# Routed experts: one accumulation array in DRAM, or two by tile parity with a sum at the end

## The reference

```python
x = x + xattn(layernorm(x), ctx_2048, Wq, bq, Wkv, bkv, Wp, bp)
flat = layernorm(x).reshape(-1, D)
scores = sqrt(softplus(flat @ router_w.T))
_, idx = top_k(scores + expert_bias, 4)
topv = take_along_axis(scores, idx, 1); topv /= topv.sum(-1) + 1e-20
probs = zeros((T, E)).at[arange(T)[:, None], idx].set(topv)
for wg, wu, wd, p in experts:
    out += p[:, None] * clamped_swiglu(flat, wg, wu, wd)
out += clamped_swiglu(flat, shared_gate_w, shared_up_w, shared_down_w)
x = x + out
```

## Time and profile before

| | |
|---|---|
| median of 3 runs | 1599.62 us |
| the profiled execution, its own time | 1606.57 us |
| its span, first to last instruction | 1604.8 us |
| mean granted TensorE clock | 0.919 |
| busy: TensorE matmul, VectorE, ScalarE, GpSimd | 83%, 65%, 53%, 53% of the span |
| DMA | 221.56 MB, mean 138 GB/s |

### The profile page before, as it was taken

One profiled execution on the slowest core, in us unless ns is written; L12 is line 12 of the kernel. 1 busy time (PEld: TensorE's weight loads), 2 busy tenths in 40 slices (PEclk: granted clock), 3 DMA queues, 4 the chain that ended last, 5 costly groups with the idle time before them and its releaser, 6 DMA issues.

```text
span 1604.8 us, 28516 instructions
## 1 busy us (share of the span) xinstructions
PE 1335.0 (83%) x7922; PEld 664.3 (41%) x7923; DVE 1036.9 (65%) x1863; ACT 851.7 (53%) x1183; POOL 855.4 (53%) x772
## 2 busy tenths in 40 slices
PE   7997787778778777887877659889988998989996
PEld 3443333344344444443443334444444444444443
DVE  6456789999999999999999827623323233332331
ACT  2223699888899888898998931112211111111221
POOL 1001477677777777777776710535444444444451
PEclk9999689898898899889898969999999999999999
DMA  7332466665666556566666647276767656666455
GB/s 225 86 72 59 73 119 125 112 119 113 129 136 130 120 118 121 118 127 131 131 115 111 115 166 250 84 229 161 198 181 213 189 129 190 162 192 129 88 93 165
DMA packets 383109, 221.56 MB, mean 138 GB/s; under 512 B 344801, under 2 KB 344929, under 8 KB 378786
## 3 DMA queue, kind: packets, MB, share of 16 engines
q1 hardware_dynamic: 365186, 177.36, 45.4%
q0 software_dynamic: 17872, 43.58, 14.3%
HBM read 103.42 MB, written 36.70 MB: 87 GB/s over the span
## 4 chain that ended last, share of the span: by engine, by line
DVE 26%; PE 25%; issue 22%; DMA 19%; ACT 4%; POOL 2%; DVEq 1%; POOLq 0%; SPq 0%; ACTq 0%
DMA acc_dram<-mem 16%; DVE mem L540 15%; PE psS L750 10%; PE psS L758 4%; DVE mem L570 3%; PE psS L434 3%; PE psAV L405 2%; PE psS L1559 2%; DMA mem<-xn_dram,mem 1%; ACT mem L493 1%; PE psT L1187 1%; PE psP L1540 1%; DMA mem<-xn_dram 1%; DVE mem L516 1%; PE psP L742 1%
## 5 line engine op out<-in xcount | busy, mean ns | idle before, releaser
L625 POOL TENSOR_SCALAR mem<-mem 128x2048 bf16<-128x2048 uint8 x256 | 485.4, 1901 | 183.6 <-DMA mem<-mem 161.5
L493 ACT ACTIVATE mem<-mem 128x2048 uint8<-128x2048 f32 x256 | 536.3, 2095 | 12.4
L434 PE MATMUL psS<-mem 128*128 128x512 bf16 x1024 | 351.6, 430 | 158.4 <-DVE mem L570 114.5
L750 PE MATMUL psS<-mem 128*128 (+1 forms) x752 | 358.4, 620 | 0.0
L570 DVE TENSOR_SCALAR_CACHE_REDUCE mem<-psS,mem 128x1024 f32<-128x1024 f32 x256 | 328.2, 1282 | 23.9
L540 DVE TENSOR_SCALAR_CACHE_REDUCE mem<-psS 128x1024 f32<-128x1024 f32 x256 | 311.9, 1218 | 18.6 <-PE psS L434 18.5
L778 ACT ACTIVATE mem<-mem 128x256 f32<-128x256 f32 x94 | 39.3, 418 | 368.2 <-DVE mem L784 368.2
L1157 POOL DMA_INDIRECT acc_dram<-mem x78 | 125.4, 1607 | 195.5 <-DVE mem L1257 152.3
L784 DVE TENSOR_SCALAR mem<-psS 128x512 f32<-128x512 f32 x94 | 65.0, 692 | 220.9 <-PE psS L750 219.4
L434 PEld LDWEIGHTS psS<-mem 128*128 128x128 bf16 x1024 | 74.2, 103 | 317.2 <-DVE mem L540 146.9
L750 PEld LDWEIGHTS psS<-mem 128*128 128x128 f32 x752 | 141.6, 199 | 149.5 <-issue 147.4
(11 more groups left out here) (207 smaller groups left out, 1253.8 us busy)
## 6 DMA issues: line engine op xcount, KB each, us to landing
mem<-in_moe_w SPq DMA_DIRECT2D x33, 1536.0 KB, 9.4
mem<-in_x SPq DMA_DIRECT2D x32, 256.0 KB, 2.9
acc_dram<-mem SPq DMA_DIRECT2D x29, 256.0 KB, 2.3
mem<-mem SPq DMA_TRANSPOSE x288, 3.1
xn_dram<-mem SPq DMA_DIRECT2D x17, 256.0 KB, 2.1
mem<-in_ctx_in SPq DMA_DIRECT2D x16, 256.0 KB, 3.2
mem<-xn_dram SPq DMA_DIRECT2D x16, 256.0 KB, 4.4
mem<-acc_dram SPq DMA_DIRECT2D x16, 256.0 KB, 4.3
```

Of the source, the lines that this page charges most:

```text
L434: last = nc.tensor.matmul(psS[c][:, k * D:(k + 1) * D], qT[p][:, h, :], kT[:, h, c * HALF + k * D:c * HALF + (k + 1) * D], start=True, sto ...
L493: nc.scalar.activation(p8[slot], S[slot], ACT.Exp, bias=NB[:, slot:slot + 1], scale=sq[p][:, h:h + 1], accum_out=Z[p][:, h:h + 1]).then_in ...
L625: nc.gpsimd.tensor_scalar(pb[slot], pT[slot].bitcast(U8).rearrange("p (j q b) -> p j b q", b=2, q=P), 1.0, 0.0, ALU.mult, ALU.add).then_in ...
L750: last = nc.tensor.matmul(bankG[o], xT[o if xo is None else xo][:, c, :], w(c * 2 * I, 2 * I), start=(c == 0), stop=(c == DC - 1))
```

## The change

There are two DRAM arrays in place of one. `residual_sum` takes the residual of attention, `shared_sum` the result of the early shared tiles; tiles 12 to 16 of `shared_sum` (16 being the spare rows) and the spare rows of `residual_sum` are zeroed at the start, by six DMAs where there was one. The early shared tiles are scaled by 1.0 out of PSUM and no residual is loaded. Routed tiles of even number are added into the first array, those of odd number into the second, and an add waits only for the one of its own parity before it (`added` is now two semaphores).

Each step's row numbers are copied by VectorE (`dve_tile_rows`), those to add to for tile k and those to gather for tile k+4 in one instruction of two columns, between `kept` and `hid`; GpSimd copies nothing. One list serves both: a pad's row lies behind the last token, where the gather's bounds check leaves it out. NT grows by 2.

At the end both arrays are loaded whole into the expert ring's space (four tiles of each, then two groups of six tiles of each), summed by VectorE and GpSimd between them (GpSimd the four late tiles and the odd early ones), and stored from SBUF. The diff, without context lines, semaphore declarations and two changed signatures:

```diff
@@ -39,7 +39,7 @@
-    NT = RT + 6
+    NT = RT + 8
@@ -49,7 +49,9 @@
-    acc_dram = nc.dram_tensor("acc_dram", (T + P, D), F32, kind="Internal").ap()
+    shared_sum = nc.dram_tensor("shared_sum", (T + P, D), F32, kind="Internal").ap()
+    residual_sum = nc.dram_tensor("residual_sum", (T + P, D), F32, kind="Internal").ap()
+    sums = (shared_sum, residual_sum)
@@ -167,15 +169,14 @@
-        from_sb, to_sb = cut(NT, I32), cut(NT, I32)
...
+        rows_sb = cut(NT, I32)
+        rows_by = rows_sb.rearrange("p (g l) -> p g l", l=MU)
...
-        x1g = [cut(D) for _ in range(MU)]
...
-        gidx = [cut(1, I32) for _ in range(MU)]
-        sidx = [cut(1, I32) for _ in range(2)]
+        tile_rows = [cut(2, I32) for _ in range(MU)]
@@ -183,7 +184,9 @@
+        late_y = [cut(D) for _ in range(LATE)]
+        again = ring.rearrange("p (s t d) -> p s t d", s=2, d=D)
@@ -688,7 +692,7 @@
-                sp.dma_start(rows(acc_dram, t - 1), x1).then_inc(x1_stored, 16)
+                sp.dma_start(rows(residual_sum, t - 1), x1).then_inc(x1_stored, 16)
...
         def pairs(eng, step):
@@ -892,8 +896,7 @@
-                dve.wait_ge(residual_in[k % MU], 16 * (k // MU + 1))
-                nc.vector.tensor_tensor(y[o], bankY[o], x1g[k % MU], ALU.add).then_inc(y_ready, 1)
+                nc.vector.tensor_scalar(y[o], bankY[o], 1.0, None, ALU.mult).then_inc(y_ready, 1)
@@ -1025,10 +1028,9 @@
-            v_.tensor_scalar(from_sb, idf, 0.0, None, ALU.max).then_inc(rows_ready, 1)
...
-            v_.scalar_tensor_tensor(to_sb, pad_of, part[:, 1:2], slotf_pad, ALU.mult, ALU.add).then_inc(rows_ready, 1)
+            v_.scalar_tensor_tensor(rows_sb, pad_of, part[:, 1:2], slotf_pad, ALU.mult, ALU.add).then_inc(rows_ready, 1)
@@ -1041,24 +1043,18 @@
             def tokens(k):
...
-            def residual(k):
-                sp.dma_start(x1g[k % MU], rows(acc_dram, k)).then_inc(residual_in[k % MU], 16)
...
-            for k in range(MU):
-                residual(k)
...
-                sp.dma_start(rows(acc_dram, k), y[k % 2]).then_inc(y_stored[k % 2], 16)
+                sp.dma_start(rows(shared_sum, k), y[k % 2]).then_inc(y_stored[k % 2], 16)
...
-                    residual(k + MU)
@@ -1087,19 +1083,32 @@
         def sp_late(sp):
...
-            end = extra * 2 + (EARLY + SURE)
-            sp.wait_ge(added, 16 * (extra * 2 + SURE))
-            apart(sp, end)
+            for o in range(2):
+                sp.wait_ge(added[o], 16 * (extra + SURE // 2))
+                apart(sp, extra)
+            def tiles(dram, first, n):
+                return dram[first * P:(first + n) * P, :].rearrange("(t p) d -> p t d", p=P)
+            for o in range(2):
+                sp.dma_start(again[:, o, EARLY:TT, :], tiles(sums[o], EARLY, LATE)).then_inc(own_again, 16)
+            part = EARLY // 2
+            for g in range(2):
+                for o in range(2):
+                    sp.dma_start(again[:, o, g * part:(g + 1) * part, :], tiles(sums[o], g * part, part)).then_inc(
+                        early_again[g], 16)
+            for g in range(2):
+                for o in range(2):
+                    sp.wait_ge(early_summed[o], (g + 1) * part // 2)
+                sp.dma_start(tiles(out, g * part, part), again[:, 0, g * part:(g + 1) * part, :]).then_inc(out_stored[0], 16)
...
-                sp.dma_start(x1g[m], rows(acc_dram, EARLY + m)).then_inc(own_again, 16)
-            sp.dma_start(out[0:EARLY * P, :], acc_dram[0:EARLY * P, :]).then_inc(out_copied, 16)
-            for m in range(LATE):
-                sp.wait_ge(y_ready, end + m + 1)
-                apart(sp, end)
-                sp.dma_start(rows(out, EARLY + m), y[m % 2]).then_inc(out_stored[m % 2], 16)
-            sp.wait_ge(out_copied, 16)
-            for o in range(2):
-                sp.wait_ge(out_stored[o], 16 * LATE // 2)
+                sp.wait_ge(out_ready, m + 1)
+                sp.dma_start(rows(out, EARLY + m), late_y[m]).then_inc(out_stored[1], 16)
+            sp.wait_ge(out_stored[0], 16 * 2)
+            sp.wait_ge(out_stored[1], 16 * LATE)
+        def early_tiles(g, odd):
+            part = EARLY // 2
+            return range(g * part + odd, (g + 1) * part, 2)
@@ -1123,43 +1132,45 @@
-            tail(eng, extra * 2 + (EARLY + SURE))
-        def pool_gather(pool, kk, l):
+            tail(eng, extra * 2 + (EARLY + SURE), extra)
+        def pool_gather(pool, l, list_column):
+            nc.gpsimd.indirect_dma_start(out=xg[l], out_offset=None, in_=xn2_dram,
+                                         in_offset=bass.IndirectOffsetOnAxis(list_column, 0),
+                                         bounds_check=T - 1, oob_is_err=False).then_inc(tokens_in[l], 16)
+        def pool_gather_next(pool, kk, l):
...
-            pool.wait_ge(tokens_tr, k - MU + 1)
+            pool.wait_ge(tile_rows_ready, k - EARLY + 1)
...
-            if not isinstance(kk, int) or kk > FIRST:
-                pool.wait_ge(share_kept, k - MU - EARLY + 1)
-                apart(pool, k)
-            nc.gpsimd.tensor_copy(gidx[l], column(from_sb, k - EARLY)).then_inc(gidx_ready, 1)
-            pool.wait_ge(gidx_ready, k - EARLY + 1)
+            pool.wait_ge(share_kept, k - EARLY + 1)
...
-            nc.gpsimd.indirect_dma_start(out=xg[l], out_offset=None, in_=xn2_dram,
-                                         in_offset=bass.IndirectOffsetOnAxis(gidx[l], 0)).then_inc(tokens_in[l], 16)
+            pool_gather(pool, l, tile_rows[l][:, 1:2])
...
         def pool_step_routed(pool, kk, l):
-            k, o = MU * kk + l, l % 2
+            k = MU * kk + l
...
-                pool_gather(pool, kk + 1, l)
-            pool_gather(pool, kk + (l + 5) // MU, (l + 1) % MU)
-            if later(kk, l - 1):
-                pool.wait_ge(added, 16 * (k - EARLY - 1))
-                apart(pool, k)
-            nc.gpsimd.tensor_copy(sidx[o], column(to_sb, k - EARLY)).then_inc(sidx_ready, 1)
-            pool.wait_ge(sidx_ready, k - EARLY + 1)
-            apart(pool, k)
-            if later(kk, l):
-                pool.wait_ge(added, 16 * (k - EARLY))
-                apart(pool, k)
+                pool_gather_next(pool, kk, l)
+            pool_gather_next(pool, kk + (l + 1) // MU, (l + 1) % MU)
...
-            nc.gpsimd.indirect_dma_start(out=acc_dram, out_offset=bass.IndirectOffsetOnAxis(sidx[o], 0), in_=y[o],
-                                         in_offset=None, compute_op=ALU.add).then_inc(added, 16)
-        def pool_tail(pool, end):
-            pool.wait_ge(added, 16 * (end - EARLY))
-            apart(pool, end)
+            o = l % 2
+            if later(kk, l - 1):
+                pool.wait_ge(added[o], 16 * ((MU // 2) * kk + (l - o - EARLY) // 2))
+                apart(pool, k)
+            nc.gpsimd.indirect_dma_start(out=sums[o], out_offset=bass.IndirectOffsetOnAxis(tile_rows[l][:, 0:1], 0),
+                                         in_=y[o], in_offset=None, compute_op=ALU.add).then_inc(added[o], 16)
+        def pool_tail(pool, end, extra):
+            for m in range(LATE):
+                pool.wait_ge(own_again, 32)
+                nc.gpsimd.tensor_tensor(again[:, 0, EARLY + m, :], again[:, 0, EARLY + m, :], again[:, 1, EARLY + m, :],
+                                        ALU.add).then_inc(late_summed, 1)
+            for g in range(2):
+                pool.wait_ge(early_again[g], 32)
+                for t in early_tiles(g, 1):
+                    nc.gpsimd.tensor_tensor(again[:, 0, t, :], again[:, 0, t, :], again[:, 1, t, :], ALU.add).then_inc(
+                        early_summed[1], 1)
@@ -1167,9 +1178,9 @@
         def pool_routed(pool):
...
+            pool.wait_ge(tokens_tr, EARLY)
...
-                pool_gather(pool, FIRST, l)
-            pool.wait_ge(rows_ready, 2)
+                pool_gather(pool, l, rows_sb[:, l:l + 1])
@@ -1248,13 +1259,24 @@
-        def dve_routed_out(dve, k, o):
+        def dve_routed_out(dve, k, o, pairs_before):
...
-            if isinstance(k, int) and k < EARLY + 2:
+            if not isinstance(k, int):
+                dve.wait_ge(added[o], 16 * pairs_before)
+            elif k < EARLY + 2:
...
-                dve.wait_ge(added, 16 * (k - EARLY - 1))
+                dve.wait_ge(added[o], 16 * pairs_before)
...
+        def dve_tile_rows(dve, kk, l):
+            k = MU * kk + l
+            if isinstance(k, int):
+                group = rows_by[:, kk - FIRST:kk - FIRST + 2, l]
+            else:
+                group = rows_by[:, bass.ds(kk - FIRST, 2), l]
+                dve.wait_ge(added[l % 2], 16 * ((MU // 2) * kk + (l - l % 2 - EARLY) // 2 - 1))
+            nc.vector.tensor_copy(tile_rows[l], group).then_inc(tile_rows_ready, 1)
...
         def dve_routed(dve, kk, l):
@@ -1266,29 +1288,46 @@
+            dve_tile_rows(dve, kk, l)
...
-                dve_routed_out(dve, k - 1, b)
-        def dve_late(dve, end):
```

(44 more changed lines are left out.)

7 lines of the change are left out of this document (4 added, 3 removed).

## The result

The change made the kernel slightly slower: 1615.48 us (median of 7 runs, 1607.72 to 1619.92) against 1601.9 (7 runs, 1597.22 to 1612.05), ratio 1.0085 [1.0053, 1.0117]. The forecast was 1575.5. The profiled execution took 1612.69 us with a span of 1611.0; before it was 1606.57 with 1604.8. From one profiled execution to the other the span grew by 6.2 us.

| part | before | after | difference | forecast |
|---|---|---|---|---|
| start to clip of tile 13 | 1064.2 | 1065.6 | +1.4 | 0 |
| 76 steps, tiles 13 to 89 | 496.5 (6.53 each) | 487.4 (6.41 each) | -9.1 | -36.7 |
| to the issue of the last add | 17.2 | 13.3 | -3.9 | -3.1 |
| to the first reload | 5.0 | 4.9 | 0 | 0 |
| to the end of the span | 22.0 | 39.7 | +17.7 | +15.6 |

What follows compares the result with a forecast made beforehand. TensorE bounds two routed stretches; between them, chained adds and late gathers hold it back. Terms -47.7 + 3 + 8 - 3.1 + 15.6 + 1 - 1 = -24.2 us, on the median's scale 1575.5 us; range 1560 to 1593.

Steps and rivals of the forecast that it cites:

- Part 1: Routed stage, tiles 13 to 89: the chain of adds goes, steps fall from 6.53 to 5.91 us; -47.7 us.
- Part 2: Routed stage: gathers and expert weights come late next, pads not gathered cost nothing; +3 us, ends 0 and +12.
- Part 3: VectorE between `kept` and `hid`: the new two-column copy delays TensorE by 0.10 us per tile; +8 us.
- Rival (a): Routed stage: VectorE's order binds, the copy costs the whole 27 us, steps 6.25 us; 1594.5 us, chance 0.08.
- Part 4: End of the routed stage: the last add is issued 3.0 us after its `y`, not 6.1; -3.1 us.
- Part 5: From first reload to end: loading, summing and storing both arrays takes 37.6 us in place of 22.0; +15.6 us.
- Part 6: Start and early stage: more zeroing and two more NT columns +1 us, no residual loads -1 us.
- (b): Routed stage: two adds in flight share transfer engines and still bind; half of 47.7 us lost, 1599.5 us, chance 0.06.
- (c): Routed stage: GpSimd binds through the gather's bounds check; at 3.5 us per gather about 1615 us, chance 0.04.
- (d): The end: transfers run at 153 to 194 GB/s and eat the gain; 1606 to 1623.5 us, chance 0.06.
- The sign that I gave a chance of 0.10: Whole kernel: the change makes it slower, against 0.84 for faster and 0.06 for the same.

Runs made afterwards that it cites:

- first edit: The changed kernel with VectorE's register load of the tile's expert number moved ahead of the clip; 1574.86 us, ratio 0.9814 to the kernel before.
- third experiment: The changed kernel with both moves: register load ahead of the clip, two-column copy behind `hid`; 1574.98 us, ratio 0.9824 to the kernel before.
- the second load: The changed kernel with load ahead of the clip, copy behind `hid`, and an extra unused load behind the clip; 1574.48 us, ratio 0.9818.
- The plain scatter: The changed kernel with scatters that overwrite rows with `y` in place of adding; 1580.17 us, ratio 0.9884 to the kernel before.

## Why the prediction was wrong

**Part 1 was right, in size too.** In the first edit 76 steps take 446.7 us; forecast from the TensorE-bound stretch were 448.9. The kernel with the adds in one chain gives 6.379, near the 6.53 of the kernel before.

**Part 2 was nothing** (+3 taken): 446.7 leaves no room for it, and the pads cost nothing either way.

**Part 3 failed, and with it the forecast.** It said that `hid` moves by 0 to 0.38 us and took 0.10 per tile, 8 us. What parts 2 and 3 were to cost together, 11 us, measured 487.4 - 448.9 = 38.5. The place was named (VectorE's order between clip and `hid`, with 0.07 us of slack), the cause wasn't. I took the 0.23 us of "issue idle" ahead of `kept` for a fixed price. It was the tail of a register load of 0.31 us and its handling, of which the rest was covered by the clip's own 0.69 us. The load's length depends on whether GpSimd issued an add 2 to 3 us earlier, and the change moved that: the median load went to 0.91 us. The 0.15 us of the copy, on which I put the price, cost nothing (first and third experiment). Rival (a) had +27 us as its whole and 1594.5 as its time; it too priced only the copy, so the measured steps pass its 6.25 too, by 0.16 each.

The trace of the kernel before could have told this: its load row has a maximum of 1.07 us above a median of 0.31, and the loads of over 0.6 us all stood 2 to 3 us behind an add. An idle put down to "issue" was read as a constant where the spread of the sequencer's own instructions should have been read.

**Part 4 was right**: -3.9 us against -3.1.

**Part 5 was near**, with errors that partly cancel: 39.7 us against 37.6. The last loads landed 25.7 us after the first reload, where 24.0 were counted; the full queues moved 388 GB/s and not 370, but the start took more than that gives back (261 GB/s from 1572 to 1576, in the trace). The last sums took 5.1 us and not 4.2, and the stores behind them 8.9 and not 9.4. The Trainium skill, page "SBUF — State Buffer", section "Who interferes with whom", says that a VectorE operation with two SBUF inputs and a GpSimd one that reads SBUF block each other. The runs agree that they slow each other: 1.35 us per VectorE sum beside GpSimd, 0.62 alone; 1.70 per GpSimd sum beside VectorE's, where its four late sums, with one operation of VectorE beside them, took 5.13 us, 1.28 each. That one waits for the other wholly isn't shown: three of 0.62 and three of 1.28 make 5.7 us one after another, and the six were done in 5.2. The Trainium skill, page "DMA: Bandwidth & Descriptors", section "Bandwidth", gives about 358 GB/s as the HBM limit per core, and says further on that this is each core's part when both cores of a pair stream, and that one alone was measured at up to 425. The 388 and 387 GB/s held for 18 us here, where the kernel runs on one core, agree with the second; the prediction set only the first against the trace.

**Part 6**: the start gave +1.4 to tile 13 where +1 and -1 were taken. That can't be told from nothing: in the traces of the edits of the changed kernel the clip of tile 13 stands anywhere from 1063.4 to 1071.7 us.

**The other rivals.** (b), adds still bind, a chance of 0.06 that the forecast called split but counted wholly as no change: no; VectorE has no wait for one. (c), GpSimd binds by its bounds check: no; a gather's issue takes 1.05 us, where it took 1.01. (d), the end at 153 to 194 GB/s: no. The sign that I gave a chance of 0.10 came about by none of them: the end took +17.7 as forecast, and the steps gave back 9.1 in place of 36.7.

**Which version is best.** The change with the load ahead of the clip: 1574.86 us, ratio 0.9814, 1.9% faster than before and, by the two ratios, 2.7% faster than the change as it was made. The versions with both moves, with all sums on VectorE and with the second load are the same within their intervals. Its ratio lies just beyond the forecast's own, 1575.5 / 1599.62 = 0.985, since part 3 was the only large miss. The closeness is partly luck: in its profiled execution the steps gave back 49.8 us and not 36.7, while tile 13 came 6.7 us later.

**What stays open.** What inside the chip holds the load isn't shown: the view has its start and end only. The plain scatter shows that the addition matters, not whether by its traffic or by the longer issue. That the changed order keeps the load in the place step after step is read from the trace and from which instruction waits for which; no run tests it by itself. Why the loads near 2.0 us end earlier is open too.

## What to carry to other kernels

An engine's program may hold a register load that nobody sees as work, since it counts as "issue idle"; where it stands between a wait and the operation that releases the bound engine, load the register ahead of the wait, where it is hidden whatever it takes. After a change of order on one engine, look at the spread of the small sequencer instructions on the others and at what was issued ahead of the longest. And where a change should have paid and did not, look for a part whose delay delays the next cause as much: one moved line was worth 40 us here.

## What the runs showed of the hardware

- A register load from SBUF takes 0.30 us on VectorE and TensorE alike, but up to 1.24 us if it begins 2 to 3 us behind the start of a scatter-add's issue on GpSimd; mostly it then ends at about 3.3 us. Behind a plain scatter 19 of 78 took over 0.36 us. Behind a gather none took over 0.33.
- Issue on GpSimd: a gather of 128 rows 1.05 us, a plain scatter 1.02, a scatter-add 1.59. In the changed kernel an add landed 4.9 us (median) after its issue.
- Two-input sums of 128x512 in f32: 0.62 us on VectorE alone; 1.35 on VectorE and 1.70 on GpSimd when both run; 1.28 on GpSimd with VectorE nearly idle.
- 387 to 388 GB/s were held while the reloads kept the queues full, and rows dropped by a bounds check saved 5.3 MB and no time.
